# Turning x for a two-layer graph network: DMA transposes replaced by TensorE transposes with a ScalarE copy

## The chip, the cores and the metric

The kernel runs on one core of a Trainium2 chip. A core has TensorE (PE) for matrix products, VectorE (DVE), ScalarE (ACT) and GpSimd (POOL) for the rest, and SyncE (SP), which here only issues DMA transfers. They run their own instruction queues in order and wait for one another through semaphores. The metric is the device time of one launch in microseconds.

## The reference, cut to what matters

Two graph layers over 4096 nodes with 512 features; `adj` is a 4096x4096 int32 matrix of 0 and 1.

```python
# layer 0
keep = (adj > 0) & (cumsum(adj > 0, axis=1) <= 64)      # the first 64 neighbours of a row
nb_mean = (keep @ x) / max(count(keep), 1)
xj = leaky_relu(nb_mean @ W_nb.T + b_nb)
xi = leaky_relu(x @ W_line.T + b_line)
h  = layernorm(x + xi + where(count(keep) > 0, xj, 0))
# layer 1
Wh = h @ W + bW
e  = leaky_relu((Wh @ a1 + b1)[:, None] + (Wh @ a2 + b2)[None, :], 0.2)
att = softmax(where(adj > 0, e, -9e15), axis=1)
out = layernorm(h + att @ Wh)
```

## The kernel before, in words

The rows are worked in T = 32 tiles of 128 (P). Three stages follow each other, each a block of code in which every engine has its own program; a stage begins on all engines when the one before has ended on all. Only the first one, the projection, is touched.

The projection computes, for every row tile t, two products with the turned x: y = x W_nb^T + b_nb, kept for the neighbour sums of the second stage, and z = x W_line^T + b_line, from which `leaky_relu(z) + x` is stored to DRAM (`r_scratch`). To keep float32 accuracy with fp16 products, every operand is split into a high fp16 part and a low one (the rest). TensorE adds the three products high*high, high*low and low*high (`PASSES`) over KB = 4 column blocks: 12 products of 128x512 for y and 12 for z, 24 in all (line 631). For them the parts of x have to lie turned, with the features on the partitions. The steps for tile t are:

- ScalarE scales x and writes the high part (`cut_x`, line 434); VectorE writes the low part (`cut_x`, line 548). Both go to `x_cut[u]`, u = t % 2.
- SP issues a transposing DMA from `x_cut[u]` to `xT[u]` (`turn_x`, line 357), 128x1024 fp16 at a time. It waits for both parts and for the products of tile t-2, which read `xT[u]` last.
- TensorE multiplies (`products`, line 631), y into PSUM bank u and z into bank 2+u.
- VectorE finishes (`finish`, lines 562 to 573): y with its scale and bias (562), z the same (567), leaky ReLU (570), plus x (573). GpSimd issues the store of the result (398).
- From step 8 on, ScalarE and VectorE also cut y of an earlier tile into two fp16 parts (lines 440 and 577): one tile a step, two a step in the last eight.

In step t, TensorE does the products of tile t, ScalarE and VectorE cut x of tile t+2, VectorE finishes tile t. In steps 0 to 6 ScalarE also sums |x| of the four tiles whose load came next (line 426), from which VectorE makes the scales. In steps 8, 10, 24, 26, 28 and 30 VectorE does a piece of the mask work of row tile 0 for the second stage (`MASK_AT`): flags, a running count (a scan along 2048 columns, line 260), values. `run_projection` writes steps 0 to 11 and 24 to 31 out and puts the ones between in a loop.

SP issues the loads of x in nine pieces. The first five go at once. The last four (`load_x(5)` and up) write where the weights lay, so they wait until these have been used, and stand between the transposes of tiles 1 to 5. The first two loads of `adj` follow. The first stores of the mask and the next loads of `adj` stand behind the last transpose.

Of the kernel before, what the change touches and what calls it, by code (L numbers as in the profile page):

```python
# [18 lines left out]
F16 = mybir.dt.float16  # L19
# [9 lines left out]
P = 128  # L29
# [10 lines left out]
def early(t, n):  # L40

    return isinstance(t, int) and t < n
# [7 lines left out]
def gnn_kernel(nc, x, adj, w_nb, b_nb, w_line, b_line, w_att, b_att, a1, b1, a2, b2, out):  # L50
# [30 lines left out]
    with ctx:  # L81
# [3 lines left out]
        def sem(name):  # L85
            return ctx.enter_context(nc.semaphore(name))
# [121 lines left out]
        x_summed, xs_ready, xmax_ready, xmax_reduced, y_scaled = sem("x_summed"), sem("xs_ready"), sem("xmax_ready"), sem("xmax_reduced"), sem("y_scaled")  # L208
        w_transposed = sem("w_transposed")
        xh_ready, xl_ready, xw_ready = sem("xh_ready"), sem("xl_ready"), sem("xw_ready")  # L210
        y_done, z_done = sem("y_done"), sem("z_done")
        x_turned = [sem(f"x_turned{u}") for u in range(2)]
        y32_ready, yh_ready, y_used = sem("y32_ready"), sem("yh_ready"), sem("y_used")
        z_ready, xi_ready, r_ready = sem("z_ready"), sem("xi_ready"), sem("r_ready")
        r_stored = [sem(f"r_stored{i}") for i in range(2)]
# [30 lines left out]
        def load_adj(sp, t, s):  # L246
            sp.dma_start(adj_in[s], adj_t[t, :, s * HALF:(s + 1) * HALF]).then_inc(adj_landed[s], 16)
# [78 lines left out]
        with nc.Block() as block:  # L326
            @block.sync
            def _(sp):
# [19 lines left out]
                load_x(2)  # L348
                load_x(3)
                load_x(4)  # L350

                def turn_x(t):
                    u = t % 2
                    sp.wait_ge(xl_ready, t + 1)
                    if t >= 2:
                        sp.wait_ge(z_done, t - 1)
                    sp.dma_start_transpose(xT[u].rearrange("p h (k i) -> p (h k) i", i=P),
                                           x_cut[u].rearrange("p h d -> p (h d)")).then_inc(x_turned[u], 16)

                for t in range(T):  # L360
                    turn_x(t)
                    if t == 1:
                        sp.wait_ge(wl_ready, 2 * KB + 1)
                        sp.wait_ge(wa_ready, 2)
                        sp.wait_ge(w_squared, 3)
                        sp.wait_ge(wline_squared, 1)
                    if t >= 1 and t + 4 < len(X_AT_ONCE) - 1:
                        sp.wait_ge(x_landed[t + 2], 16)
                        load_x(t + 4)
                    if t == 5:  # L370
                        sp.wait_ge(x_landed[len(X_AT_ONCE) - 2], 16)
                        load_adj(sp, 0, 0)
                        load_adj(sp, 0, 1)
                for s in range(2):
                    sp.wait_ge(m_ready, s + 1)
                    sp.dma_start(m_dram[0, :, s * HALF:(s + 1) * HALF], m_half[s]).then_inc(m_stored[s], 16)
# [32 lines left out]
            def _(act):  # L409
# [18 lines left out]
                def cut_x(t, u):  # L428
                    if beyond(t, T):
                        return  # L430
                    act.wait_ge(xs_ready, x_group(t) + 1)
                    if not early(t, 2):
                        act.wait_ge(x_turned[u], 8 * (t - u))
                    nc.scalar.activation(x_cut[u][:, 0, :].unsqueeze(1), x_slot(t), ACT.Copy, scale=xs[:, bass.ds(t, 1)]).then_inc(xh_ready, 1)

                def cut_y(t):
                    act.wait_ge(y_scaled, 1)
# [16 lines left out]
                cut_x(0, 0)  # L454
                cut_x(1, 1)
                sums_x(2, 2)
                nc.scalar.activation(watt[:, 0, :, 0:D], watt_in, ACT.Copy, scale=sc[:, S_W + 2:S_W + 3]).then_inc(wh_ready, 1)
                nc.scalar.activation(watt[:, 0, :, D:D + 2], wa32[:], ACT.Copy, scale=sc[:, S_W + 3:S_W + 4]).then_inc(wh_ready, 1)

                def step(t, u):  # L460
                    cut_x(t + 2, u)
                    if early(t, 7):
                        sums_x(4 + 4 * t, 4)
                    if is_step(t, 7):
                        act.wait_ge(bias_landed, 2 * 16)
                        nc.scalar.activation(junk_a[:, D:2 * D], bnb_bc, ACT.Square, accum_out=ssw[:, 4:5]).then_inc(w_squared, 1)
                        act.wait_ge(w_squared, 4)
                        nc.scalar.activation(bound[:, 4:5], ssw[:, 4:5], ACT.Sqrt).then_inc(root_ready, 1)
                    for c in tiles_to_cut(t):
                        cut_y(c)  # L470
# [4 lines left out]
            def _(dve):  # L475
# [66 lines left out]
                def cut_x(t, u):  # L542
                    if beyond(t, T):
                        return
                    dve.wait_ge(xh_ready, t + 1)
                    if not early(t, 2):
                        dve.wait_ge(x_turned[u], 8 * (t - u))
                    nc.vector.scalar_tensor_tensor(out=x_cut[u][:, 1, :].unsqueeze(1), in0=x_slot(t), scalar=xs[:, bass.ds(t, 1)],
                                                   in1=x_cut[u][:, 0, :].unsqueeze(1), op0=ALU.mult, op1=ALU.subtract).then_inc(xl_ready, 1)

# [62 lines left out]
            def _(pe):  # L613
                pe.wait_ge(idents_ready, 6)
                pe.wait_ge(w_landed, 2 * 16)
                for n in range(2 * KB):
# [2 lines left out]
                        last = nc.tensor.transpose(bank[n][:, c * P:(c + 1) * P], src[:, c, (n % KB) * P:(n % KB + 1) * P], ident[:, :])  # L619
                    last.then_inc(w_transposed, 1)  # L620

                def products(t, u):
                    if beyond(t, T):
                        return
                    pe.wait_ge(x_turned[u], 8 * (t - u) + 16)
                    if not early(t, 2):
                        pe.wait_ge(z_ready, t - 1)
                    for w, b, done in ((wnb_T, u, y_done), (wline_T, 2 + u, z_done)):
# [4 lines left out]
                        last.then_inc(done, 1)  # L633

                def step(t, u):
                    products(t, u)

                pe.wait_ge(wl_ready, 2 * KB)
                run_projection(pe, step)

# [698 lines left out]
```

## Time and profile before

| | us |
|---|---|
| median of 3 runs (1662.28 to 1664.14) | 1662.72 |
| the profiled execution | 1662.72 |
| its span in the trace | 1661.0 |
| TensorE busy, of the span | 1518.9 |
| VectorE busy, of the span | 1461.2 |
| ScalarE busy, of the span | 1024.8 |
| the products of line 631, 768 of them | 174.2 |

The span is the time from the first to the last instruction in the trace. Busy times are of one engine and overlap with those of the others. The mean of one product in a list (391 ns for line 631) is longer than its place in the stream, as products overlap; the length of an unbroken piece over its count tells the place. A duration behind a row of several instructions is that of the whole piece. The granted clock is 1.00 when TensorE has its full 2.4 GHz and 0.50 at 1.2 GHz.

### The profile page before, as it was taken

The page shows a single profiled execution, that of the slowest core. Times are in us where ns is not written, and L with a number is a line of the kernel's source. Part 1 is how long each engine was busy: PE and PEld are TensorE (multiplying, and loading weights), DVE is VectorE, ACT ScalarE, POOL GpSimd, SP SyncE. Part 2 cuts the span into 40 slices and gives each one's busy share as a digit, 9 for nine tenths or more (in the row PEclk, how much of TensorE's full clock was granted, in tenths as well). Part 3 has the DMA queues.
Part 4 walks back from the last instruction along what each step waited for, and adds up shares of the span by engine and source line. Part 5 has one row for each costly group of instructions (what it writes and reads, how often), then busy time and mean ns, then how long its engine had stood idle before and what let it go on. Part 6 is the DMA issues. An engine that isn't in the chain of part 4 may idle for free. (4 is left out here: it accounts for less than half of the span.)

```text
span 1661.0 us, 30461 instructions
## 1 busy us (share of the span) xinstructions
PE 1518.9 (91%) x11296; PEld 934.1 (56%) x11296; DVE 1461.2 (88%) x1687; ACT 1024.8 (62%) x1489; POOL 141.6 (9%) x117
## 2 busy tenths in 40 slices
PE   2799969999998989898999799999999999999996
PEld 1344425555554545454556467677777676767664
DVE  4688999999999999999994599889899999999782
ACT  5422325555555556565555368678787878796973
POOL 0011100111111111111110000000000000000000
PEclk8999979999999999999999999999999999999998
DMA  6733355555454545555442311112131212130101
GB/s 221 228 96 101 96 164 179 178 178 176 164 181 156 177 165 177 177 177 170 164 166 105 108 51 52 52 46 100 45 101 51 101 51 101 49 103 26 62 27 51
DMA packets 115429, 198.14 MB, mean 119 GB/s; under 512 B 41264, under 2 KB 74032, under 8 KB 107184
## 3 DMA queue, kind: packets, MB, share of 16 engines
q1 hardware_dynamic: 108352, 173.31, 32.9%
q0 software_dynamic: 7024, 24.12, 3.7%
q8 instruction: 34, 0.56, 0.1%
q14 instruction: 19, 0.16, 0.0%
HBM read 130.29 MB, written 58.72 MB: 114 GB/s over the span
## 5 line engine op out<-in xcount | busy, mean ns | idle before, releaser
L873 PE MATMUL psum<-reg_ab,reg_c 128*128 128x512 f16 x2048 | 472.6, 388 | 0.0
L1279 PE MATMUL psum<-reg_ab 128*128 128x385 f16 x1024 | 335.0, 327 | 7.4 <-DVE reg_ab L1161 5.4
L1280 PE MATMUL psum<-reg_ab 128*128 128x384 f16 x1024 | 334.4, 327 | 0.0
L1281 PE MATMUL psum<-reg_ab 128*128 128x385 f16 x1024 | 334.4, 327 | 0.0
L873 PEld LDWEIGHTS psum<-reg_ab,reg_c 128*128 128x128 f16 x2048 | 200.3, 100 | 230.3 <-issue 19.5
L1019 ACT ACTIVATE reg_ab<-reg_ab,reg_c 128x512 f32<-128x512 f32 x256 | 170.1, 712 | 115.5 <-DVE reg_ab L1147 115.3
L631 PE MATMUL psum<-reg_ab 128*128 128x512 f16 x768 | 174.2, 391 | 24.3 <-DMA reg_ab<-reg_ab 24.3
L1293 PE MATMUL psum<-reg_ab 128*128 128x128 f16 x1024 | 178.5, 219 | 0.0
L1292 PE MATMUL psum<-reg_ab 128*128 128x128 f16 x1024 | 178.5, 219 | 0.0
L1294 PE MATMUL psum<-reg_ab 128*128 128x128 f16 x1024 | 178.4, 218 | 0.0
L1147 DVE TENSOR_TENSOR reg_ab<-reg_ab 128x1024 f32<-128x1024 f32 x128 | 156.4, 1222 | 22.9 <-ACT reg_ab L1011 22.9
L1011 ACT ACTIVATE reg_ab<-reg_ab,reg_c 128x512 f32<-128x512 f32 x256 | 169.6, 710 | 0.0
L1161 DVE TENSOR_TENSOR reg_ab<-reg_ab 128x1024 f16<-128x1024 f32 x128 | 156.1, 1220 | 5.6 <-ACT reg_ab L1026 5.4
L1154 DVE SCALAR_TENSOR_TENSOR reg_ab<-reg_ab 128x1024 f32<-128x1024 f32 x128 | 156.2, 1220 | 0.3 <-ACT reg_ab L1019 0.3
L267 DVE SCALAR_TENSOR_TENSOR reg_c<-reg_c 128x2048 f16<-128x2048 bf16 x64 | 146.4, 2288 | 3.3
L740 ACT ACTIVATE reg_c<-psum,small 128x1024 f16<-128x1024 f16 x128 | 141.8, 1108 | 9.9 <-PE psum L862 9.9
L631 PEld LDWEIGHTS psum<-reg_ab 128*128 128x128 f16 x768 | 76.4, 100 | 121.8 <-issue 21.5
L260 DVE TENSOR_TENSOR_SCAN reg_c<-reg_c,small 128x2048 bf16<-128x2048 uint8 x32 | 143.5, 4484 | 1.1
L723 POOL TENSOR_TENSOR xx<-xx,batt_bc 128x512 f32<-128x512 f32 x32 | 95.7, 2992 | 567.9 <-DVE h_cut L822 567.9
L1026 ACT ACTIVATE reg_ab<-reg_ab 128x1024 f16<-128x1024 f32 x128 | 133.5, 1043 | 16.4 <-PE psum L1294 16.3
L260 DVE TENSOR_TENSOR_SCAN reg_c<-reg_c 128x2048 bf16<-128x2048 uint8 x32 | 141.5, 4423 | 0.1
L1281 PEld LDWEIGHTS psum<-reg_ab 128*128 128x128 f16 x1024 | 99.7, 97 | 68.3 <-issue 0.9
(149 smaller groups left out, 2096.6 us busy)
## 6 DMA issues: line engine op xcount, KB each, us to landing
reg_c<-in_adj SPq DMA_DIRECT2D x64, 1024.0 KB, 5.6
m_scratch<-reg_c SPq DMA_DIRECT2D x64, 256.0 KB, 2.3
wt_scratch<-reg_c SPq DMA_DIRECT2D x128, 128.0 KB, 1.8
reg_ab<-wt_scratch SPq DMA_DIRECT2D x32, 512.0 KB, 3.5
reg_c<-m_scratch SPq DMA_DIRECT2D x28, 512.0 KB, 4.0
r_scratch<-reg_ab POOLq DMA_DIRECT2D x32, 256.0 KB, 2.3
r_in<-r_scratch SPq DMA_DIRECT2D x32, 256.0 KB, 2.8
hb_scratch<-xx POOLq DMA_DIRECT2D x32, 256.0 KB, 4.3
```

Source lines behind the costliest of these rows:

```text
L260: nc.vector.tensor_tensor_scan(cum, m_half[s], m_half[s], carry[:, 0:1] if s else 0.0, ALU.add, ALU.max).then_inc(cum_ready, 1)
L631: last = nc.tensor.matmul(bank[b][:, :], xT[u][:, hx, k * P:(k + 1) * P], w[:, hw, k, :], start=(k == 0 and (hx, hw) == PASSES[0]), stop=( ...
L873: last = nc.tensor.matmul(bank[u][:, :], keepT[u][:, j * P:(j + 1) * P], y_parts[:, j, part, :], start=(j == 0 and part == 0), stop=(j == ...
L1011: ins = nc.scalar.activation(e[:, :, jj, :], A1_bc.rearrange("p (k i) -> p k i", i=P), ACT.Identity, bias=b2col[:, 1, g * JG + jj:g * JG + ...
L1019: ins = nc.scalar.activation(e[:, :, jj, :], e[:, :, jj, :], ACT.Exp, bias=b2col[:, 0, g * JG + jj:g * JG + jj + 1])
L1147: nc.vector.tensor_tensor(e, A2, e, ALU.max).then_inc(u_ready, 1)
L1279: nc.tensor.matmul(bank[k][:, 0:D + 1 - P], h, v_rows[:, j, P:D + 1], start=(g == 0 and jj == 0), stop=False, skip_group_check=True)
L1280: nc.tensor.matmul(bank[k][:, 0:D - P], h, v_low[:, j, P:D], start=False, stop=False, skip_group_check=True)
L1281: last = nc.tensor.matmul(bank[k][:, 0:D + 1 - P], l, v_rows[:, j, P:D + 1], start=False, stop=end, skip_group_check=True)
L1292: nc.tensor.matmul(acc, h, v_high[:, j, 0:P], start=(g == 0 and jj == 0 and k == 0), stop=False, skip_group_check=True)
L1293: nc.tensor.matmul(acc, h, v_low[:, j, 0:P], start=False, stop=False, skip_group_check=True)
L1294: last = nc.tensor.matmul(acc, l, v_high[:, j, 0:P], start=False, stop=(g == G - 1 and jj == JG - 1 and k == CT - 1), skip_group_check=True)
```

## The change

The transposing DMA goes. In its place TensorE turns x itself, in `transpose_x`: 8 transposes of 128x128 fp16 against an identity matrix, into PSUM bank 4+u read as fp16, which are followed by one ScalarE copy of 128x1024 fp16 from there to `xT[u]` (`copy_xT`). TensorE turns tile t+1 at the head of step t, ahead of the products of tile t. ScalarE copies tile t+1 in step t, behind its cut of tile t+2. `x_cut[u]` is free for tile t+2 when the transposes of tile t are done. The loads of x and `adj` on SP are issued in a row, with the same waits as before but without the transposes between them.

```diff
--- before.py
+++ after.py
@@ -208,8 +208,7 @@
         x_summed, xs_ready, xmax_ready, xmax_reduced, y_scaled = sem("x_summed"), sem("xs_ready"), sem("xmax_ready"), sem("xmax_reduced"), sem("y_scaled")
         w_transposed = sem("w_transposed")
         xh_ready, xl_ready, xw_ready = sem("xh_ready"), sem("xl_ready"), sem("xw_ready")
-        y_done, z_done = sem("y_done"), sem("z_done")
-        x_turned = [sem(f"x_turned{u}") for u in range(2)]
+        x_transposed, xT_ready, y_done, z_done = sem("x_transposed"), sem("xT_ready"), sem("y_done"), sem("z_done")
         y32_ready, yh_ready, y_used = sem("y32_ready"), sem("yh_ready"), sem("y_used")
         z_ready, xi_ready, r_ready = sem("z_ready"), sem("xi_ready"), sem("r_ready")
         r_stored = [sem(f"r_stored{i}") for i in range(2)]
@@ -348,29 +347,16 @@
                 load_x(2)
                 load_x(3)
                 load_x(4)
-
-                def turn_x(t):
-                    u = t % 2
-                    sp.wait_ge(xl_ready, t + 1)
-                    if t >= 2:
-                        sp.wait_ge(z_done, t - 1)
-                    sp.dma_start_transpose(xT[u].rearrange("p h (k i) -> p (h k) i", i=P),
-                                           x_cut[u].rearrange("p h d -> p (h d)")).then_inc(x_turned[u], 16)
-
-                for t in range(T):
-                    turn_x(t)
-                    if t == 1:
-                        sp.wait_ge(wl_ready, 2 * KB + 1)
-                        sp.wait_ge(wa_ready, 2)
-                        sp.wait_ge(w_squared, 3)
-                        sp.wait_ge(wline_squared, 1)
-                    if t >= 1 and t + 4 < len(X_AT_ONCE) - 1:
-                        sp.wait_ge(x_landed[t + 2], 16)
-                        load_x(t + 4)
-                    if t == 5:
-                        sp.wait_ge(x_landed[len(X_AT_ONCE) - 2], 16)
-                        load_adj(sp, 0, 0)
-                        load_adj(sp, 0, 1)
+                sp.wait_ge(wl_ready, 2 * KB + 1)
+                sp.wait_ge(wa_ready, 2)
+                sp.wait_ge(w_squared, 3)
+                sp.wait_ge(wline_squared, 1)
+                for q in range(5, len(X_AT_ONCE) - 1):
+                    sp.wait_ge(x_landed[q - 2], 16)
+                    load_x(q)
+                sp.wait_ge(x_landed[q], 16)
+                load_adj(sp, 0, 0)
+                load_adj(sp, 0, 1)
                 for s in range(2):
                     sp.wait_ge(m_ready, s + 1)
                     sp.dma_start(m_dram[0, :, s * HALF:(s + 1) * HALF], m_half[s]).then_inc(m_stored[s], 16)
@@ -430,8 +416,16 @@
                         return
                     act.wait_ge(xs_ready, x_group(t) + 1)
                     if not early(t, 2):
-                        act.wait_ge(x_turned[u], 8 * (t - u))
+                        act.wait_ge(x_transposed, t - 1)
                     nc.scalar.activation(x_cut[u][:, 0, :].unsqueeze(1), x_slot(t), ACT.Copy, scale=xs[:, bass.ds(t, 1)]).then_inc(xh_ready, 1)
+
+                def copy_xT(t, u):
+                    if beyond(t, T):
+                        return
+                    act.wait_ge(x_transposed, t + 1)
+                    if not early(t, 2):
+                        act.wait_ge(z_done, t - 1)
+                    nc.scalar.activation(xT[u].rearrange("p h d -> p (h d)"), bank[4 + u][:, :].bitcast(F16), ACT.Copy).then_inc(xT_ready, 1)
 
                 def cut_y(t):
                     act.wait_ge(y_scaled, 1)
@@ -454,11 +448,13 @@
                 cut_x(0, 0)
                 cut_x(1, 1)
                 sums_x(2, 2)
+                copy_xT(0, 0)
                 nc.scalar.activation(watt[:, 0, :, 0:D], watt_in, ACT.Copy, scale=sc[:, S_W + 2:S_W + 3]).then_inc(wh_ready, 1)
                 nc.scalar.activation(watt[:, 0, :, D:D + 2], wa32[:], ACT.Copy, scale=sc[:, S_W + 3:S_W + 4]).then_inc(wh_ready, 1)
 
                 def step(t, u):
                     cut_x(t + 2, u)
+                    copy_xT(t + 1, 1 - u)
                     if early(t, 7):
                         sums_x(4 + 4 * t, 4)
                     if is_step(t, 7):
@@ -544,7 +540,7 @@
                         return
                     dve.wait_ge(xh_ready, t + 1)
                     if not early(t, 2):
-                        dve.wait_ge(x_turned[u], 8 * (t - u))
+                        dve.wait_ge(x_transposed, t - 1)
                     nc.vector.scalar_tensor_tensor(out=x_cut[u][:, 1, :].unsqueeze(1), in0=x_slot(t), scalar=xs[:, bass.ds(t, 1)],
                                                    in1=x_cut[u][:, 0, :].unsqueeze(1), op0=ALU.mult, op1=ALU.subtract).then_inc(xl_ready, 1)
 
@@ -619,10 +615,22 @@
                         last = nc.tensor.transpose(bank[n][:, c * P:(c + 1) * P], src[:, c, (n % KB) * P:(n % KB + 1) * P], ident[:, :])
                     last.then_inc(w_transposed, 1)
 
+                def transpose_x(t, u):
+                    if beyond(t, T):
+                        return
+                    pe.wait_ge(xl_ready, t + 1)
+                    if not early(t, 2):
+                        pe.wait_ge(xT_ready, t - 1)
+                    dst = bank[4 + u][:, :].bitcast(F16)
+                    for h in range(2):
+                        for k in range(KB):
+                            last = nc.tensor.transpose(dst[:, h * D + k * P:h * D + (k + 1) * P], x_cut[u][:, h, k * P:(k + 1) * P], ident16[:, :])
+                    last.then_inc(x_transposed, 1)
+
                 def products(t, u):
                     if beyond(t, T):
                         return
-                    pe.wait_ge(x_turned[u], 8 * (t - u) + 16)
+                    pe.wait_ge(xT_ready, t + 1)
                     if not early(t, 2):
                         pe.wait_ge(z_ready, t - 1)
                     for w, b, done in ((wnb_T, u, y_done), (wline_T, 2 + u, z_done)):
@@ -633,9 +641,11 @@
                         last.then_inc(done, 1)
 
                 def step(t, u):
+                    transpose_x(t + 1, 1 - u)
                     products(t, u)
 
                 pe.wait_ge(wl_ready, 2 * KB)
+                transpose_x(0, 0)
                 run_projection(pe, step)
 
 
```

TensorE's queue at the start of the products, before: there is nothing but groups of 24 products (the first row of a group with its waits, then the other 23).

```order
L631 MATMUL psum<-reg_ab 128x512 [waits x_turned0,wl_ready]
L631 MATMUL psum<-reg_ab 128x512 x23
L631 MATMUL psum<-reg_ab 128x512 [waits x_turned1]
L631 MATMUL psum<-reg_ab 128x512 x23
L631 MATMUL psum<-reg_ab 128x512 [waits z_ready,x_turned0]
L631 MATMUL psum<-reg_ab 128x512 x23
L631 MATMUL psum<-reg_ab 128x512 [waits z_ready,x_turned1]
L631 MATMUL psum<-reg_ab 128x512 x23
```

The changed kernel, the same place. `ident16` is the identity matrix; line 627 is a transpose, line 639 a product.

```order
L627 MATMUL psum<-ident16,reg_ab 128x128 [waits xl_ready,wl_ready]
L627 MATMUL psum<-ident16,reg_ab 128x128 x7
L627 MATMUL psum<-ident16,reg_ab 128x128 [waits xl_ready]
L627 MATMUL psum<-ident16,reg_ab 128x128 x7
L639 MATMUL psum<-reg_ab 128x512 [waits xT_ready]
L639 MATMUL psum<-reg_ab 128x512 x23
L627 MATMUL psum<-ident16,reg_ab 128x128 [waits xT_ready,xl_ready]
L627 MATMUL psum<-ident16,reg_ab 128x128 x7
L639 MATMUL psum<-reg_ab 128x512 [waits xT_ready]
L639 MATMUL psum<-reg_ab 128x512 x23
L627 MATMUL psum<-ident16,reg_ab 128x128 [waits xT_ready,xl_ready]
L627 MATMUL psum<-ident16,reg_ab 128x128 x7
```

Each group of 24 products now has a group of 8 transposes ahead of it, of the next tile, and that waits for the low cut of the next tile (`xl_ready`), behind which the products of the present tile stand.

SP's queue from the first transpose on, before:

```order
L357 DMA_TRANSPOSE reg_ab<-reg_ab 128x8x128 [waits xl_ready] x2
L337 DMA reg_ab<-in_x 128x4x512 [waits wline_squared,w_squared,x_landed3,wa_ready,wl_ready]
L357 DMA_TRANSPOSE reg_ab<-reg_ab 128x8x128 [waits z_done,xl_ready]
L337 DMA reg_ab<-in_x 128x4x512 [waits x_landed4]
L357 DMA_TRANSPOSE reg_ab<-reg_ab 128x8x128 [waits z_done,xl_ready]
L337 DMA reg_ab<-in_x 128x4x512 [waits x_landed5]
L357 DMA_TRANSPOSE reg_ab<-reg_ab 128x8x128 [waits z_done,xl_ready]
L337 DMA reg_ab<-in_x 128x4x512 [waits x_landed6]
L357 DMA_TRANSPOSE reg_ab<-reg_ab 128x8x128 [waits z_done,xl_ready]
L247 DMA reg_c<-in_adj 128x2048 [waits x_landed8]
L247 DMA reg_c<-in_adj 128x2048
L357 DMA_TRANSPOSE reg_ab<-reg_ab 128x8x128 [waits z_done,xl_ready] x26
L376 DMA m_scratch<-reg_c 128x2048 [waits m_ready]
```

The changed kernel, the same place:

```order
L336 DMA reg_ab<-in_x 128x4x512 [waits wline_squared,w_squared,x_landed3,wa_ready,wl_ready]
L336 DMA reg_ab<-in_x 128x4x512 [waits x_landed4]
L336 DMA reg_ab<-in_x 128x4x512 [waits x_landed5]
L336 DMA reg_ab<-in_x 128x4x512 [waits x_landed6]
L246 DMA reg_c<-in_adj 128x2048 [waits x_landed8]
L246 DMA reg_c<-in_adj 128x2048
L362 DMA m_scratch<-reg_c 128x2048 [waits m_ready]
```

Four x loads, two loads of `adj` and the first mask store now stand one behind the other; the 32 transposes between them are gone.

ScalarE's queue in steps 0 and 1, before (line 434 is the high cut, 426 the sum of |x|, 457 and 458 the cut of the second layer's weights):

```order
L457 ACTIVATE watt<-reg_ab,sc 128x4x512
L458 ACTIVATE watt<-wa32,sc 128x4x2
L434 ACTIVATE reg_ab<-reg_ab,reg_c 128x512 [waits x_turned0,xs_ready]
L426 ACTIVATE reg_c<-reg_ab 128x512 [waits x_summed,x_landed2]
L426 ACTIVATE reg_c<-reg_ab 128x512 [waits x_summed] x3
L434 ACTIVATE reg_ab<-reg_ab,reg_c 128x512 [waits x_turned1,xs_ready]
L426 ACTIVATE reg_c<-reg_ab 128x512 [waits x_summed,x_landed3]
L426 ACTIVATE reg_c<-reg_ab 128x512 [waits x_summed] x3
```

The changed kernel, from the copy of tile 0 on (line 428 is the copy, 420 the high cut, 412 the sum):

```order
L428 ACTIVATE reg_ab<-psum 128x1024 [waits x_transposed]
L452 ACTIVATE watt<-reg_ab,sc 128x4x512
L453 ACTIVATE watt<-wa32,sc 128x4x2
L420 ACTIVATE reg_ab<-reg_ab,reg_c 128x512 [waits x_transposed,xs_ready]
L428 ACTIVATE reg_ab<-psum 128x1024 [waits x_transposed]
L412 ACTIVATE reg_c<-reg_ab 128x512 [waits x_summed,x_landed2]
L412 ACTIVATE reg_c<-reg_ab 128x512 [waits x_summed] x3
L420 ACTIVATE reg_ab<-reg_ab,reg_c 128x512 [waits x_transposed,xs_ready]
L428 ACTIVATE reg_ab<-psum 128x1024 [waits z_done,x_transposed]
L412 ACTIVATE reg_c<-reg_ab 128x512 [waits x_summed,x_landed3]
L412 ACTIVATE reg_c<-reg_ab 128x512 [waits x_summed] x3
```

Each step has one more instruction, which stands behind the cut of the tile after and ahead of the sums.

## Rows read from the trace of the kernel before

**Rows 1.** Busy us by stretch: stretch, length, PE, PEld, DVE, ACT, POOL, clock, DMA.
```profile
53.70:116.40 62.70, 59.95 (x264) 26.32 (x264) 46.06 (x84) 25.60 (x59) 5.33 (x10) 0.96 0.58 168
...
177.30:226.00 48.70, 40.94 (x175) 17.46 (x173) 47.17 (x70) 12.14 (x19) 4.52 (x8) 0.93 0.45 130
...
229.30:870.00 640.70, 579.00 (x3802) 325.22 (x3803) 619.19 (x624) 372.92 (x477) 108.23 (x58) 0.97 0.52 172
```

**Rows 2.** Timeline, TensorE, first stage: start, us, operation, idle before and releaser.
```profile
34.66 12.47 PE L631 MATMUL psum<-reg_ab 128*128 128x512 f16 x48 [11.29 <-DMA reg_ab<-reg_ab]
53.76 23.52 PE L631 MATMUL psum<-reg_ab 128*128 128x512 f16 x96 [6.64 <-DMA reg_ab<-reg_ab]
79.20 36.43 PE L631 MATMUL psum<-reg_ab 128*128 128x512 f16 x168 [1.92 <-DMA reg_ab<-reg_ab]
116.43 93.55 PE L631 MATMUL psum<-reg_ab 128*128 128x512 f16 x432 [0.80 <-DMA reg_ab<-reg_ab]
213.63 8.25 PE L631 MATMUL psum<-reg_ab 128*128 128x512 f16 x24 [3.65 <-DMA reg_ab<-reg_ab]
```

**Rows 3.** Waits before 260 us: total, times, longest.
```profile
PE psum L631 <- DMA reg_ab<-reg_ab: 24.3, 5, 11.3
```

**Rows 4.** Timeline, VectorE, the stage's tail.
```profile
178.80 0.75 DVE L567 SCALAR_TENSOR_TENSOR reg_ab<-psum,reg_c,reg_ab 128x512 f32<-128x512 f32 x1 [0.74 <-PE psum L631]
...
184.64 0.74 DVE L548 SCALAR_TENSOR_TENSOR reg_ab<-reg_ab,reg_c 128x512 f16<-128x512 f32 x1
...
190.85 0.74 DVE L567 SCALAR_TENSOR_TENSOR reg_ab<-psum,reg_c,reg_ab 128x512 f32<-128x512 f32 x1
...
209.71 0.75 DVE L548 SCALAR_TENSOR_TENSOR reg_ab<-reg_ab,reg_c 128x512 f16<-128x512 f32 x1
...
215.27 0.74 DVE L567 SCALAR_TENSOR_TENSOR reg_ab<-psum,reg_c,reg_ab 128x512 f32<-128x512 f32 x1
...
222.49 0.75 DVE L567 SCALAR_TENSOR_TENSOR reg_ab<-psum,reg_c,reg_ab 128x512 f32<-128x512 f32 x1
...
224.60 1.41 DVE L577 SCALAR_TENSOR_TENSOR reg_ab<-reg_ab,sc 128x512 f16<-128x512 f32 x2
```

**Rows 5.** Timeline, start of the product loop.
```profile
30.39 0.74 DVE L548 SCALAR_TENSOR_TENSOR reg_ab<-reg_ab,reg_c 128x512 f16<-128x512 f32 x1
...
31.16 2.73 SPq L357 DMA_TRANSPOSE reg_ab<-reg_ab  x2
...
46.63 0.74 DVE L548 SCALAR_TENSOR_TENSOR reg_ab<-reg_ab,reg_c 128x512 f16<-128x512 f32 x1
...
58.57 0.61 ACT L426 ACTIVATE reg_c<-reg_ab 128x512 f32<-128x512 f32 x1
...
59.31 0.63 ACT L426 ACTIVATE reg_c<-reg_ab 128x512 f32<-128x512 f32 x1
```

**Rows 6.** Timeline, stage 2, around one set of transposes.
```profile
504.35 0.62 PE L913 MATMUL psum<-ident,h_cut 128*128 128x128 f16 x8 [2.53 <-DVE h_cut L822]
...
504.81 0.61 PE L862 MATMUL psum<-ident,reg_c 128*128 128x128 f16 x8
...
505.01 1.02 ACT L783 ACTIVATE hT<-psum 128x1024 f16<-128x1024 f16 x1 [0.33 <-PE psum L913]
...
505.26 3.62 PE L873 MATMUL psum<-reg_ab,reg_c 128*128 128x512 f16 x16
```

**Rows 7.** Timeline, TensorE, stage 2, sets after an idle time.
```profile
270.93 1.03 PE L913 MATMUL psum<-ident,h_cut 128*128 128x128 f16 x8 [3.14 <-DVE h_cut L822]
...
397.46 1.03 PE L913 MATMUL psum<-ident,h_cut 128*128 128x128 f16 x8 [2.54 <-DVE h_cut L822]
...
399.14 4.26 PE L873 MATMUL psum<-reg_ab,reg_c 128*128 128x512 f16 x16
```

**Rows 8.** Timeline, VectorE, steps 10 and 11 of the product loop.
```profile
105.31 0.75 DVE L567 SCALAR_TENSOR_TENSOR reg_ab<-psum,reg_c,reg_ab 128x512 f32<-128x512 f32 x1 [0.21 <-PE psum L631]
...
112.54 0.75 DVE L548 SCALAR_TENSOR_TENSOR reg_ab<-reg_ab,reg_c 128x512 f16<-128x512 f32 x1
```

## The prediction

> **What bounds the kernel now.** I read the engine shares, then busy time by stretch, then the waits of the first stage, then TensorE's and VectorE's order of time in it. The diff touches only the first stage, from the start to 226.0 us. Behind it VectorE is busy 619.19 of 640.70 us [rows 1]: the second stage hangs on VectorE, nothing in it changes, and it starts when the first ends. So the question is by how much VectorE's last instruction of the first stage moves. M(t) are the 24 products of row tile t, T(t) its 8 new transposes, D(t) VectorE's low cut of tile t (L548).
>
> TensorE runs the M's in five unbroken pieces [rows 2]: M(0) and M(1) from 34.66, M(2) to M(5) from 53.76, M(6) to M(12) from 79.20, M(13) to M(30) from 116.43, M(31) from 213.63. In the long pieces 432 products take 93.55 us, 0.2165 each, so 5.20 per M. The transposing DMA holds TensorE up 24.3 us in all [rows 3], in the gaps 11.29, 6.64, 1.92, 0.80 and 3.65 before those pieces [rows 2] (the first is mostly setup). Between 53.7 and 116.4 VectorE is busy only 46.06 of 62.70 us, so TensorE leads; from 177.3 it is busy 47.17 of 48.70 [rows 1], because each step cuts two y tiles and four steps carry mask work. So the stage's end is VectorE's queue from its last long wait, for the second product of tile 24 at 178.80, to its last y cut, 224.60 and 1.41 [rows 4].
>
> **The change.** It takes 32 DMA transposes (3.5 us from the first issue, 31.16, to the product that needed it, 34.66 [rows 2, 5]) out of the chain and puts in 32 sets of 8 TensorE transposes and 32 ScalarE copies of 128x1024 fp16. It also unties the x loads on SP's queue from the transposes.
>
> *Price of a set.* The same form stands in stage 2: h_cut's set starts at 504.35, the next set at 504.81, the product behind at 505.26 [rows 6]. That is 0.46 and 0.45; I take 0.46, so a TensorE step becomes 5.66. The bounds are 0.45 and 0.62 (a set to its modelled end, if what follows had to wait for it). A set costs nothing only where TensorE waits anyway.
> The Trainium skill ("TensorE: Matmul & The Clock Gate", Part 4: PE-mode transpose) gives about 275 ns for one transpose inside a kernel and says such work does not count as busy for the clock gate. The rows disagree on the first: 57 ns from start to start. By the page a set would be 2.2 us (an estimate from its figure), and the sum would be a rival, below. On the second no row here speaks, since no transposes run alone for long.
>
> *Price of a copy.* The copy of hT, same shape, takes 1.02 us [rows 6]. ScalarE is busy 25.60 of 62.70 us [rows 1]; eleven more copies make 37. In the steps with four |x| sums (58.57 to 59.31, 0.74 from start to start [rows 5]) the order is cut, no more than 0.75 either, copy 1.0, sums 3.0: some 4.8, under 5.66. copy(t+1) runs beside M(t). So copies cost nothing; the cover would be gone if a step's ScalarE work passed 5.66.
>
> *Start.* T(0) can start behind D(0), 30.39+0.74, at 31.2. The clock is then at its lower level, 1.2 GHz: two sets took 399.14-397.46=1.68 there [rows 7], 0.84 each. Result at about 32.3, copy to 33.3, M(0) at 33.4 instead of 34.66, T(1) done in between. M(0) and M(1) are 12.3 long to their last issue, plus one set: M(1) ends at 46.2. T(3) wants D(3), which stood at 46.63 behind VectorE's finish of tile 0 and the cut of watt [rows 5]; these move with M(0), so D(3) ends near 46.2, T(3) stands at 46.3 and M(2) at 46.8, against 53.76. There the DMA and the restart at the lower clock both go: M(2) to M(5) ended at 53.76+23.52=77.28, 2.7 us more than 4 x 5.20.
> The x loads on SP no longer alternate with transposes, and the first two mask stores, queued behind all 32 of them before, may leave as soon as the masks are made; nothing in this stage waits for those. The tile-16 group goes out at about 45.6 instead of 46.8; ScalarE summed it from 58.57 before without waiting, so it lands in under 11.8, by 57.4. ScalarE is there at 55.9: the scales for tile 4 come near 49.5, then two cuts (0.7), two copies (1.0) and four sums (0.75). Even 1.2 us of wait there is covered, as cut and D of tile 6 are then ready at 62.2 and T(6) stands at 63.3.
>
> *Middle.* M(10) starts at 46.8+8x5.66=92.1 (before: 79.20+4x5.20=100.0). Tile 10's second product was taken by VectorE at 105.31, 5.31 after M(10)'s start; now 97.4. Behind it come the rest of finish, the scan, a y cut, and D(13) to 112.54+0.75, that is 7.98 later [rows 8]: now 105.4. T(13) stands ahead of M(12) in TensorE's queue, where the DMA stood ahead only of M(13): the lead is partly lost. M(11) ends at 102.9, so TensorE waits 2.5, then M(12) starts at 105.95 and M(13) at 111.6 (before 116.43). Eleven steps on, M(24) starts at 111.6+11x5.66=173.9, before 116.43+11x5.20=173.6. The 4.8 us of lead are used up by 11 x 0.46=5.1: +0.25.
>
> *Tail.* VectorE takes tile 24 at 179.05 instead of 178.80 and then is the longer queue. D(27) ends at 185.38+0.25=185.6 [rows 4]; T(27) ahead of M(26) waits 1.0 for it (M(25) ends 184.7), M(26) starts at 186.15, its second product is there at 191.46 where VectorE wants it at 190.85+0.25: +0.35. D(31) ends 209.71+0.75+0.6=211.05. M(29) ends at 186.15+3x5.66+5.20=208.3, so T(31) waits 2.8 (the trace would show 2.65 idle), M(30) starts at 211.55 and tile 30 is there at 216.86, wanted at 215.27+0.6: +1.0. M(31), about 217.2 to 222.4, is in time for VectorE (222.49+1.6). Sum: 0.25+0.35+1.0=+1.6 us.
>
> *Clock.* At an idle of 2.53 before T-like sets the clock stayed up (504.35: 8 in 0.46 us [rows 6]), at 2.54 it was down once and at 3.14 too (397.46, 270.93: 8 in 1.03 [rows 7]). My 2.5 and 2.65 lie beside the first, so I take 0. The upper end, each: 2.9, as M(31) took 8.25 against 5.36 after 3.65 idle [rows 2]. The nearer price for a piece that begins with a set: two sets lose 1.68-0.91=0.8, and 16 products took 4.26 against 3.62 [rows 6, 7], 1.4; I use 2.1, the middle.
>
> The profiled run took 1662.72 us, which is also the median of the three; its span is 1661.0. Forecast: 1662.72+1.6=**1664.3**.
>
> **Rivals.**
> B, the clock falls in one of the two new waits (before T(13) or T(31)): +1.6+2.1=+3.7, 1666.4; in both, +5.8, 1668.5. For it: 397.46 and 270.93, and the wait for T(31) lies between the rows. Against: 504.35. This is the case on the other side: slower by over 0.2% once one wait costs more than 1.7 us.
> C, a set costs 0.62: 8 sets before M(10) and 11 after M(13), 19x0.16=3.0 more, 1667.3. For it: every set stands between products that use other operands. Against: 504.81 to 505.26, which is just such a passage.
> D, the tail starts earlier than I say: T(0) begins 2.2 us ahead of M(0) and may have brought the clock up, and M(0) with M(1) took 12.47 against 48x0.2165+0.16=10.55 [rows 2], so up to 1.9 go; all that follows is tied to it, and if the waits for tiles 26 and 30 close too, another 1.35: 1661.0. Against: the set before M(0) is short, and VectorE's tail itself gets no shorter.
> E, the skill's price: 2.2-0.46=1.74 for about 28 sets, 49 us, less the 6.3 of waits of TensorE that they would fill: about 1707. The same 57 ns speak against it.
>
> **How the numbers follow.** Forecast case A 0.42, its own range 1662.5 to 1666.0; B 0.36, C 0.10, D 0.08, E 0.01, and 0.03 for a gain that I don't see. The measurement tells about 0.2% (3.3 us) from no change, that is 1659.4 to 1666.0. Faster: the 0.03 and 0.02 of D, 0.05. Slower: of A 0.03, of B 0.23 (one fall sits on the bound), of C 0.08, E 0.01, together 0.35. Same: the rest, 0.60. The range holds A, B and C and nearly all of D: 1660.8 to 1669.0.
>
> **What would show it.** First product at 33.4 and M(2) at about 46.8, no idle of 6.64. Steps of 5.66 between M(2) and M(11) (start to start). A wait of about 2.5 for D(13) before T(13), at 103, and about 2.7 before T(31), at 208; M(24) within 1 us of 173.9; VectorE's last row of the stage ending at 227.6. Granted clock 1.00 in 103 to 112 and 211 to 217 says A, about half says B. I am wrong if steps take over 5.7, if ScalarE's copy becomes what M(t) waits for, if M(2) stays behind 49, or if anything behind 230 us changes its length.

## The result, and the profile after

The kernel with the change took 1686.74 us (median of 4 runs, 1686.09 to 1691.83) against 1663.43 beside it: 1.0139 times as long, interval 1.0116 to 1.0163. That is slower, and outside the range given. The profiled execution spans 1687.5 us against 1661.0, 26.5 more. It is one of the longer ones (1689.05 us), so what follows splits 26.5 us, while the medians are 23.3 apart.

The timeline of TensorE in the first stage after the change (columns: start, duration, engine, line, operation, tiles, count, idle before it and what ended it). L627 are the new transposes, L639 the products:

```profile
32.02 1.86 PE L627 MATMUL psum<-ident,reg_ab 128*128 128x128 f16 x16 [6.72 <-DVE reg_ab L544]
34.15 7.43 PE L639 MATMUL psum<-reg_ab 128*128 128x512 f16 x24 [0.26 <-ACT reg_ab L428]
...
47.53 5.34 PE L639 MATMUL psum<-reg_ab 128*128 128x512 f16 x24
...
98.17 5.34 PE L639 MATMUL psum<-reg_ab 128*128 128x512 f16 x24
105.95 0.62 PE L627 MATMUL psum<-ident,reg_ab 128*128 128x128 f16 x8 [2.44 <-DVE reg_ab L544]
106.41 7.03 PE L639 MATMUL psum<-reg_ab 128*128 128x512 f16 x24
...
175.62 5.34 PE L639 MATMUL psum<-reg_ab 128*128 128x512 f16 x24
...
187.63 0.62 PE L627 MATMUL psum<-ident,reg_ab 128*128 128x128 f16 x8 [1.05 <-DVE reg_ab L544]
...
213.58 1.03 PE L627 MATMUL psum<-ident,reg_ab 128*128 128x128 f16 x8 [3.17 <-DVE reg_ab L544]
214.41 12.94 PE L639 MATMUL psum<-reg_ab 128*128 128x512 f16 x48
```

The waits for the transposing DMA [rows 2, 3] are gone, and the three waits for VectorE's low cut stand ahead of the tiles for which they were forecast, 13, 27 and 31. VectorE's last instruction of the stage, from its timeline (it answers to the last of [rows 4]):

```profile
231.32 1.41 DVE L573 SCALAR_TENSOR_TENSOR reg_ab<-reg_ab,sc 128x512 f16<-128x512 f32 x2
```

The stage ends at 232.7 instead of 226.0: 6.7 of the 26.5 us. The first product of the third stage, from TensorE's timelines before and after the change:

```profile
955.91 0.48 PE L1279 MATMUL psum<-reg_ab 128*128 128x385 f16 x1 [5.44 <-DVE reg_ab L1161]
```

```profile
962.93 0.48 PE L1289 MATMUL psum<-reg_ab 128*128 128x385 f16 x1 [5.44 <-DVE reg_ab L1171]
```

From the end of the first stage (226.0 and 232.7) to it are 729.9 and 730.2 us, so the second stage is 0.3 us longer. The other 19.4 us go in the third, which the diff does not touch. There TensorE runs a hardware loop over chunks 1 to 6 (`pe.Fori(1, NCH - 1)`), six passes with five jumps back. ScalarE makes the same copy once a pass, behind the pass's last products; before, from its timeline:

```profile
1133.44 0.60 ACT L1045 ACTIVATE reg_c<-psum 128x512 f32<-128x512 f32 x1 [0.85 <-PE psum L1294]
...
1219.41 0.60 ACT L1045 ACTIVATE reg_c<-psum 128x512 f32<-128x512 f32 x1 [0.85 <-PE psum L1294]
```

A pass is 85.97 us, each of them, and TensorE goes from one into the next without a hole (the last product of one, the first of the next, its timeline before):

```profile
1133.19 0.22 PE L1294 MATMUL psum<-reg_ab 128*128 128x128 f16 x1
1133.24 0.33 PE L1279 MATMUL psum<-reg_ab 128*128 128x385 f16 x1
```

After the change the passes are 91.29, 88.86, 89.15, 89.1 and 90.93, together 19.4 more. The chain of waits after the change (columns: start, duration, what held it) has at each jump a piece that belongs to nothing:

```profile
1140.46 0.61 ACT reg_c L1055
1141.07 2.81 issue
1143.89 0.33 PE psum L1289
...
1231.75 0.61 ACT reg_c L1055
1232.36 2.07 issue
...
1320.61 0.61 ACT reg_c L1055
1321.22 2.27 issue
...
1409.76 0.61 ACT reg_c L1055
1410.37 2.21 issue
...
1498.86 0.61 ACT reg_c L1055
1499.47 2.46 issue
```

"issue" means that the engine waited for nothing that the profile shows. The last of them begins when ScalarE's copy at 1498.86 has ended. TensorE had been idle a little longer each time, as its last product was done before that copy. The waits of TensorE from 1050 to 1655 us sum the whole idle time at the five jumps, called holes from here on (us, count, longest):

```profile
PE psum L1289 <- issue: 15.0, 5, 3.5
```

The rest is 19.4-15.0=4.4; 3.7 of it lie in the first and the fifth pass, whose beginning has a lower clock. Windows behind the first, the second and the fifth jump after the change (columns: us, then busy time and count of PE, PEld, DVE, ACT, POOL, then granted clock, DMA share, GB/s):

```profile
1143.80:1149.00 5.20, 5.11 (x21) 2.63 (x22) 5.20 (x5) 5.20 (x8) 0.00 (x0) 0.67 0.51 173
1234.40:1239.60 5.20, 5.17 (x47) 3.59 (x48) 5.20 (x6) 5.20 (x8) 0.00 (x0) 1.00 0.32 107
...
1502.40:1507.60 5.20, 5.20 (x25) 2.70 (x23) 5.20 (x6) 5.07 (x8) 0.00 (x0) 0.67 0.31 104
```

Behind the first hole the clock is down for a while and 21 products run in a stretch that holds 47 behind the second. The two passes that begin with a low clock are the long ones, by 5.32 and 4.96 us, with holes of 3.5 and 3.1. The other three are longer by 2.89 to 3.18, with holes of 2.7 to 2.9.

One more number moved. The DMA queue that carries the instructions themselves (packets, MB, share), in the third stage alone, first before (945 to the end), then after:

```profile
q8 instruction: 19, 0.31, 0.2%
```

```profile
q8 instruction: 64, 1.05, 0.6%
```

45 packets more: nine for each jump back.

### The profile page after: what moved, and what is told of

It is laid out like the page before. It is cut to its first block and busy times, and to the rows that moved or that the text cites. A ratio compares the mean times of both kernels' runs of the same rounds, so it can differ in the third digit from the quotient of the medians.

```text
span 1687.5 us, 31015 instructions
## 1 busy us (share of the span) xinstructions
PE 1539.6 (91%) x11552; PEld 951.6 (56%) x11552; DVE 1461.6 (87%) x1687; ACT 1056.1 (63%) x1521; POOL 141.8 (8%) x117
## 3 DMA queue, kind: packets, MB, share of 16 engines
q8 instruction: 81, 1.33, 0.3%
## 5 line engine op out<-in xcount | busy, mean ns | idle before, releaser
L639 PE MATMUL psum<-reg_ab 128*128 128x512 f16 x768 | 177.0, 389 | 0.3 <-ACT reg_ab L428 0.3
L1289 PEld LDWEIGHTS psum<-reg_ab 128*128 128x128 f16 x1024 | 99.4, 97 | 86.0 <-issue 24.1
L1291 PEld LDWEIGHTS psum<-reg_ab 128*128 128x128 f16 x1024 | 100.1, 98 | 68.9 <-issue 1.9
```

The lines of the kernel that those rows point to most:

```text
L639: last = nc.tensor.matmul(bank[b][:, :], xT[u][:, hx, k * P:(k + 1) * P], w[:, hw, k, :], start=(k == 0 and (hx, hw) == PASSES[0]), stop=( ...
L1289: nc.tensor.matmul(bank[k][:, 0:D + 1 - P], h, v_rows[:, j, P:D + 1], start=(g == 0 and jj == 0), stop=False, skip_group_check=True)
L1291: last = nc.tensor.matmul(bank[k][:, 0:D + 1 - P], l, v_rows[:, j, P:D + 1], start=False, stop=end, skip_group_check=True)
```

## The experiments

The theory after this reading: TensorE holds its program in a store of limited size that is filled in blocks. The loop's body is 1610 instructions of TensorE; before, the theory goes, it lay so in the blocks that all of it stayed held from pass to pass; the change puts 374 instructions in front of it (22 sets are written out, the rest run through a loop; each has 8 transposes, 8 weight loads and a wait that was not there), which moves it against the blocks' edges, and now it is fetched anew at each jump. The rival: something of the first stage's new order or data reaches the third (the clock, a queue, the x loads). Semaphore increments on a semaphore that nobody waits for, put at the head of TensorE's program, move the loop and take some time at the start. A loop is called clean below when it has no holes.

**The change with 138 increments at the head of TensorE's program** (374+138=512):

```
+                for _ in range(138):
+                    pe.sem_inc(filler, 1)
```

> The changed kernel with 138 semaphore increments at the head of TensorE's program, where TensorE idles until the weights land, so that all its later instructions stand 138 places further on; nothing else changes. Theory 1 (code position): the third stage's loop on TensorE, 1610 instructions long, now lies where its code is loaded again at every jump back; before it lay 374 instructions earlier, and 374+138=512=2x256, so it lies as before relative to blocks of 256. Then the five waits of 2 to 3 us behind the jumps and the short ones between go, some 18 us, and about +6.7 of the first stage stay: 1669 to 1671, and instruction packets on queue 8 fall from 81 to about 35. Theory 2 (the added transposes or what they leave behind slow the third stage by themselves): no change, 1686 to 1688, 81 packets.

Measured: 1665.09 (11 runs) against 1662.22, ratio 1.0016 [1.0006, 1.0026], less than the 1669 to 1671 expected; why is told with the clock below. The instruction queue over the whole span, before, after the change, and here:

```profile
q8 instruction: 34, 0.56, 0.1%
```

```profile
q8 instruction: 81, 1.33, 0.3%
```

```profile
q8 instruction: 36, 0.59, 0.1%
```

The same copies on ScalarE's timeline here:

```profile
1135.88 0.60 ACT L1057 ACTIVATE reg_c<-psum 128x512 f32<-128x512 f32 x1 [0.85 <-PE psum L1306]
...
1221.85 0.60 ACT L1057 ACTIVATE reg_c<-psum 128x512 f32<-128x512 f32 x1 [0.85 <-PE psum L1306]
```

85.97 again. There are more instructions than in the change alone and the time is 21.6 us less: the loss hangs on where the loop lies, not on what the change does.

**The kernel before with 118 increments** (374-256=118), the same two lines with 118:

> The kernel before with 118 semaphore increments at the head of TensorE's program (118=374-256, so its third-stage loop lies relative to blocks of 256 as in the changed kernel). Theory 1 (code position): the first two stages stay as they are, the third gets the loads behind every jump: 1679 to 1683, about 80 instruction packets on queue 8. Theory 2 (the transposes' own effect): 1663, 34 packets.

Measured: 1684.39 (5 runs), ratio 1.0143 [1.012, 1.0166], with nothing of the change in it, 1.4 us above the expected range. Its instruction queue, its waits of TensorE in the loop (the sixth is a short one behind the second jump):

```profile
q8 instruction: 80, 1.31, 0.3%
```

```profile
PE psum L1281 <- issue: 15.2, 6, 3.5
```

Its passes are 91.33, 89.29, 89.08, 90.93 and 89.15 us, together 19.9 above five of 85.97. So 118 idle instructions make the whole loss of the third stage. The rival falls. Here the clock is low (0.67) behind the first and the fourth jump.

**The kernel before with 256 increments:**

> The kernel before with 256 such increments, more than in the run with 118. Theory 1 (position within a block of 256): 1662 to 1665, as without them, 34 or 35 instruction packets. A rival, that any longer TensorE program costs (the increments themselves, or a longer program ahead of the loop): more than with 118, so 1681 or above. Theory 2: 1663.

Measured: 1683.5 (5 runs), ratio 1.0127 [1.0111, 1.0144]. The total missed, the mechanism did not. The instruction queue, and TensorE's and VectorE's timelines in the first stage:

```profile
q8 instruction: 35, 0.57, 0.1%
```

```profile
40.41 6.11 PE L621 MATMUL psum<-ident,reg_ab 128*128 128x128 f32 x32 [40.41 <-issue]
```

```profile
243.67 1.41 DVE L577 SCALAR_TENSOR_TENSOR reg_ab<-reg_ab,sc 128x512 f16<-128x512 f32 x2
```

The loop is clean (no hole, one packet more), but the increments themselves took until 40.41, 0.158 us each, and TensorE's first instruction, a transpose of the weights, stood at 17.91 before. The stage ended 19.1 us later. The 118 and 138 of the other runs ended at 19.10 and 22.15; that put the first transpose off by 1.2 and 3.5 us, but not the first product (34.65 against 34.66, and 33.95 against 34.15).

**The kernel before with 70 and with 100 increments,** one run each, to find the edge:

> The kernel before with 70 increments. Counted by its instructions, the loop of 1610 needs 7 blocks of 256 when it begins within the first 182 places of a block, else 8. The second packet pattern of the kernel before (next load 4.7 us after the last jump) puts its beginning near place 54 to 94, so with 70 more it still fits: about 35 packets, no waits behind the jumps, 1662 to 1668. If any shift costs: 80 packets and 1680.

> The same with 100 increments: place 154 to 194, around the edge of 182. Either 35 packets and 1662 to 1668 or 80 packets and 1680 to 1685; nothing in between if what decides is whether one more block is touched. If the cost grows with the shift, a value in between, with some 55 packets.

Measured: 1662.51 with 34 packets, and 1692.46 with 80 and passes of 90.35 to 92.12 us. The edge lies between. The second is above the 1680 to 1685 expected. Its holes are 15.4 us in all, as in the others, but the clock was low behind all five of them; the window behind the second:

```profile
1229.60:1234.80 5.20, 5.16 (x17) 2.43 (x18) 5.20 (x5) 5.20 (x8) 0.00 (x0) 0.50 0.35 107
```

So what a hole costs differs by what the clock does behind it.

**The change with the loop written out:**

```
-                with pe.Fori(1, NCH - 1) as c:
+                for c in range(1, NCH - 1):
```

> The changed kernel, without increments, with TensorE's third-stage loop over six chunks written out (the other engines keep their loops). Theory 1 (the jump back goes to code that is no longer held): without a jump all code comes in order, ahead of its use, so no waits of 2 to 3 us at the chunk borders: 1664 to 1671 (as the run shifted by 138), with more instruction packets than any run so far, about 120 on queue 8. If loading code costs by its amount (the path cannot keep up, or the loads disturb), as slow as the changed kernel or slower: 1686 or above.

Measured: 1665.16 (11 runs) against 1662.44, ratio 1.0016 [1.0007, 1.0025], all passes 85.97. Without a jump there is no hole, though every block comes in for the first time. The count of packets was forecast wrong:

```profile
q8 instruction: 67, 1.10, 0.3%
```

It is 31 above the 36 of the run with 138 increments, and five more copies of the body are 5x1610=8050 instructions, so a packet of 16.4 KB (1.33 MB over 81) holds about 8050/31=260 instructions, and 256 increments leave the loop clean; both fit blocks of 256.

**The change with a shorter body,** 32 of each chunk's products left out in chunks 1 to 6, without and with the 138 increments:

```
+                            if isinstance(c, int) or g not in (2, 4, 6, 8):
+                                nc.tensor.matmul(acc, h, v_low[:, j, 0:P], ...)
```

> The changed kernel at its own place, without increments, but in TensorE's third-stage loop (chunks 1 to 6) 32 products of 128x128 (high part of the weights times low part of V, first 128 columns, groups 2, 4, 6 and 8) are left out; they are 64 instructions of 1610, and the place where the loop begins stays. The runs shifted by 70 and 100 put the edge so that the changed kernel's loop is 18 to 48 instructions too long for 7 blocks. If the number of blocks that the loop touches decides, 1546 instructions fit: no waits behind the jumps, about 35 packets on queue 8, and 1665 less 6x32x0.056=10.7, 1652 to 1657. If the place of its beginning decides by itself, the waits stay: 1672 to 1677 and some 80 packets.

> The same with the 138 increments, as what the shorter loop costs where it surely fits: 1652 to 1657, about 35 packets, under either theory.

Measured, one run each: 1659.2 with 35 packets, 1660.57 with 36, and no hole in either. So a body that is shorter runs clean without being moved. The saving was forecast too large: a pass is still 85.5 us, and TensorE, busy 84.3 of them, now waits for ScalarE (6.5 us in six waits from 1050 to 1655), while half of the chain of waits in a pass (42 us) runs over VectorE. That VectorE is the new bound is likely, and not shown.

**A version that avoids what the first stage lost.** T(t+1) is put behind the first twelve products of M(t) (those for y) instead of ahead of all 24, so that it asks for VectorE's cut 2.6 us later, with the 138 increments, and then without them and with the loop written out:

```
                         last.then_inc(done, 1)
+                        if b == u:
+                            transpose_x(t + 1, 1 - u)
 ...
-                    transpose_x(t + 1, 1 - u)
                     products(t, u)
```

> The changed kernel with the transposes of tile t+1 between the y and the z products of tile t instead of ahead of both, and with the 138 increments. If the rest of the first stage's loss is the order in TensorE's queue (transposes that wait for VectorE's low cut hold up products that are ready), the waits of 2.4, 1.1 and 3.2 us before tiles 13, 27 and 31 fall to 0, 0 and about 1, the clock stays up, and the stage ends some 2 us before that of the kernel before (226.0): 1660 to 1663 with theory 1 right for the third stage. If each set costs by itself what the first stage lost, it ends where the changed kernel's does, 1669 to 1671. With theory 1 wrong add 18 to either.

> The order with the transposes between the y and the z products, and TensorE's third-stage loop written out, no increments. Theory 1: as the run with 138 increments and this order, 1657 to 1661. If code loading by its amount costs: 1675 or above.

Measured: 1659.36 (8 runs), ratio 0.9975 [0.9965, 0.9986], and 1659.72 (11 runs), 0.998 [0.9971, 0.9989]: both beat both kernels. The first is just below the 1660 to 1663 expected, the second inside its range. TensorE's timeline of the first has no wait at tile 13 and a short one at tile 31, and the stage ends at 224.1; that wait, and VectorE's last row of the stage:

```profile
208.85 0.62 PE L629 MATMUL psum<-ident,reg_ab 128*128 128x128 f16 x8 [1.03 <-DVE reg_ab L544]
```

```profile
222.71 1.41 DVE L573 SCALAR_TENSOR_TENSOR reg_ab<-reg_ab,sc 128x512 f16<-128x512 f32 x2
```

## Why the prediction was wrong

**The step that failed** is in its first paragraph: the second stage "hangs on VectorE, nothing in it changes", and by the same silence the third. The sum took what lies behind the diff to keep its length. It named the sign ("if anything behind 230 us changes its length"), but gave it no price and no chance. The instruction count of the edit, 374 on TensorE, could have been set against a loop of 1610 further down and the queue that carries instructions; none of the five cases held that. What the runs showed in its place: the jumps of the third stage's loop now fetch its code again, 15.0 us of holes and 4.4 behind them. 19.4 of the 26.5 us are this.

**The first stage, by its steps.** Price of a set: right, a step is 5.63 against 5.66 (each of the steps from 47.53 to 98.17). Copies at nothing: right, no M waits for ScalarE but the first, 0.26. Start: forecast 33.4 for M(0), 34.15 came; M(2) 46.8, 47.53 came. Wait before T(13): 2.5, 2.44 came. Wait before T(27): 1.0, 1.05. Wait before T(31): 2.65 as shown, 3.17 came. M(24): 173.9, 175.62 came. M(12) was 0.46 late (106.41 for 105.95) and took 1.69 longer at the lower clock (7.03 for 5.34); the shorter steps gave 0.4 back.

**The clock** is a second term that the sum had wrong. Case A took 0, B 2.1 for each fall. In the profiled run it fell at both: M(12) takes 7.03 instead of 5.34, 1.7 more; the set at 213.58 takes 1.03 instead of 0.62, and M(30) with M(31) 12.94 against 10.52 with 138 increments, 2.8 more together. The same windows as forecast, after the change and then with 138 increments:

```profile
103.00:112.00 9.00, 6.56 (x30) 2.65 (x29) 7.59 (x11) 2.25 (x3) 0.54 (x1) 0.81 0.08 29
211.00:217.00 6.00, 3.42 (x15) 1.75 (x16) 5.93 (x10) 2.24 (x3) 0.06 (x1) 0.62 0.00 0
```

```profile
103.00:112.00 9.00, 6.76 (x30) 3.23 (x31) 7.10 (x11) 2.24 (x3) 0.54 (x1) 0.81 0.08 30
211.00:217.00 6.00, 4.14 (x26) 2.12 (x27) 5.93 (x11) 2.24 (x3) 0.54 (x1) 1.00 0.00 0
```

The forecast read 1.00 as A and half as B: B, in both waits, and its +5.8 stands beside the +6.7 measured. But after the same idle of 3.17 us the clock is down in one run and up in the other, which has one fall, at T(13), and ends the stage at 229.2, +3.2 beside B's +3.7. With the loop written out it is the other way round: no fall after 2.44 us of idle (1.00), one after 3.16 (0.56), and the stage ends at 229.6, +3.6. So each of these three runs had a fall in one of the two waits, or in both. With the loop back in place, the change costs 2.9 us (1665.09-1662.22) or 2.7 (1665.16-1662.44), between A's 1.6 and B's 3.7. This is also why the run with 138 increments came out below its 1669 to 1671, which had taken over the +6.7. The runs don't say on what the clock decides.

**The rivals.** C is refuted (0.45 for a set in the middle), D did not come, E neither: the new rows have 0.45 from the first of eight transposes to the product behind them, 56 ns each. The page that E rested on (the Trainium skill's "TensorE: Matmul & The Clock Gate", Part 4) has 275 ns as the duration of one; the trace has 219 ns for that at the full clock (the least, the median and the longest of all, the last at the lower clock):

```profile
L627 PE MATMUL psum<-ident,reg_ab x256: 219/219/311, 32.0 to 214.3; 128*128 128x128 f16 x128
```

## What to carry to other kernels

An edit that adds instructions to an engine moves every hardware loop behind it in that engine's program. Count the loop's body: where it is long (here 1610 instructions, clean in seven blocks of 256 and not in eight), look at the packets of the instruction queue in the stretch of the loop, before and after, and test with idle instructions at the head before judging the edit by its time. A step that is put ahead of other work waits for its own input there, and holds up the work behind it: half a step later it cost nothing, and the kernel was 2.9 us faster than before instead of 2.9 slower.

## What the runs showed of the hardware

- Where a loop of 1610 instructions lies in TensorE's program is worth 1.4%: 118 idle increments ahead of it made the kernel before 22 us slower (1684.39 against 1662.22).
- A jump back that came with nine packets of instructions left a hole of 3.0 us on TensorE (15.0 over 5). Behind two of five such holes (0.67 in the window after the change and with 118 increments), and behind all five with 100 increments (0.50 to 0.74), the clock was lower for a while.
- Semaphore increments on TensorE's queue took at most 0.158 us each (40.41 us for 256; 118 ended at 19.10, so 138 more took 21.3, 0.154 each).
- An idle of 3.17 us left the granted clock at 1.00 in one run and at 0.62 in another. One of 2.44 us left it at 1.00 with the loop written out, and the window behind it has 0.81 after the change and with 138 increments.
- Eight fp16 transposes of 128x128 on TensorE follow each other every 56 ns, while one takes 219 ns from start to end.
